# Attention stage: GpSimd's sums and lower halves of the key and query products spread over several units, finishing steps moved to units 68 to 79, output weights loaded before the key stores

## The reference

```
a1 = attn(q, k1, v1, causal=True)      # latent
a2 = attn(q, ks, vs, causal=False)     # 64 selected tokens
a3 = attn(q, kw, vw, causal=True)      # window
out = g[:,0]*a1 + g[:,1]*a2 + g[:,2]*a3
```

## Time and profile before

| | us |
|---|---|
| median of 3 runs | 2634.81 (2633.99 to 2637.43) |
| the profiled execution, its own time | 2636.5 |
| its span in the profile | 2634.8 |
| PE busy (PEld busy) | 2237.9 (1863.9) |
| DVE, ACT, POOL busy | 1877.2, 1720.0, 1758.6 |

### The profile page before, as it was taken

One profiled execution on the slowest core, in us unless ns is written; L12 is line 12 of the kernel. 1 busy time (PEld: TensorE's weight loads), 2 busy tenths in 40 slices (PEclk: granted clock), 3 DMA queues, 4 the chain that ended last, 5 costly groups with the idle time before them and its releaser, 6 DMA issues. The chain is left out here.

```text
span 2634.8 us, 37397 instructions
## 1 busy us (share of the span) xinstructions
PE 2237.9 (85%) x11394; PEld 1863.9 (71%) x11394; DVE 1877.2 (71%) x3720; ACT 1720.0 (65%) x3574; POOL 1758.6 (67%) x1544
## 2 busy tenths in 40 slices
PE   0178578999999999999999999999999994839885
PEld 0165437887878788787878878788888883728885
DVE  2656467687887878787787878788888873555553
ACT  3433216787877878777787777788888883216663
POOL 4154516778787877878787787877878774017884
PEclk9975569999999999999999999999999997759998
DMA  9767726345252434425342542322412203426776
GB/s 380 327 204 236 224 62 166 75 91 133 62 137 74 93 86 96 119 75 134 77 93 76 107 111 63 94 43 55 80 34 55 44 16 87 140 83 189 194 197 169
DMA packets 199860, 314.81 MB, mean 119 GB/s; under 512 B 95915, under 2 KB 130219, under 8 KB 186731
## 3 DMA queue, kind: packets, MB, share of 16 engines
q1 hardware_dynamic: 189947, 298.23, 40.6%
q0 software_dynamic: 9712, 14.18, 2.9%
HBM read 210.20 MB, written 101.75 MB: 118 GB/s over the span
## 5 line engine op out<-in xcount | busy, mean ns | idle before, releaser
L1418 POOL TENSOR_TENSOR p_lo<-prob,p_hi 128x512 fp32r<-128x512 f32 (+3 forms) x1072 | 1232.6, 1169 | 396.6 <-ACT p_hi L1502 368.4
L1500 ACT ACTIVATE prob<-ps_s 128x512 f32<-128x512 f32 (+4 forms) x1344 | 727.2, 541 | 380.8 <-DVE ps_s L1736 208.8
L1502 ACT ACTIVATE p_hi<-ps_s 128x512 fp32r<-128x512 f32 (+3 forms) x1344 | 726.3, 540 | 1.6
L1634 DVE TENSOR_REDUCE max_part<-ps_x 128x1 f32<-128x512 f32 x744 | 506.7, 687 | 108.5 <-PE ps_x L1546 98.2
L1632 DVE CUSTOM_DVE_ANT_0 ps_x<-ps_x,before 128x128 f32<-128x128 f32 x496 | 244.0, 492 | 30.5 <-PE ps_x L1546 22.0
L1599 PE MATMUL ps_o<-p_hi,v_lat 128*128 128x512 f32 (+3 forms) x640 | 240.3, 376 | 26.0 <-POOL p_lo L1418 25.9
L1599 PE MATMUL ps_o<-p_hi,v_win 128*128 128x512 f32 (+3 forms) x640 | 238.0, 372 | 2.7 <-POOL p_lo L1418 2.7
L1601 PE MATMUL ps_o<-p_lo,v_lat 128*128 128x512 f32 (+3 forms) x640 | 237.8, 372 | 0.0
L1601 PE MATMUL ps_o<-p_lo,v_win 128*128 128x512 f32 (+3 forms) x640 | 235.2, 367 | 0.0
L1418 DVE TENSOR_TENSOR p_lo<-prob,p_hi 128x512 fp32r<-128x512 f32 (+1 forms) x208 | 207.7, 999 | 10.8 <-ACT p_hi L1502 10.7
L1736 DVE TENSOR_TENSOR ps_s<-ps_s,mask_kq 128x128 f32<-128x128 f32 x512 | 150.2, 300 | 74.2 <-PE ps_s L1518 65.6
(11 more groups left out here) (433 smaller groups left out, 5823.6 us busy)
## 6 DMA issues: line engine op xcount, KB each, us to landing
raw<-in_experts_w_dram SPq DMA_DIRECT2D x23, 1536.0 KB
wbuf<-in_tok_weight_dram SPq DMA_DIRECT2D x16, 2000.0 KB, 16.9
head_first<-kw_scratch SPq DMA_DIRECT2D x72, 256.0 KB, 5.0
kw_scratch<-st_hi SPq DMA_DIRECT2D x48, 256.0 KB, 2.3
kw_scratch<-st_lo SPq DMA_DIRECT2D x48, 256.0 KB, 3.0
q_scratch<-st_hi SPq DMA_DIRECT2D x48, 256.0 KB, 4.4
q_scratch<-st_lo SPq DMA_DIRECT2D x48, 256.0 KB, 5.1
head_first<-q_scratch SPq DMA_DIRECT2D x48, 256.0 KB, 6.0
```

Of the source, the lines that this page charges most:

```text
L1418: ns.tensor_tensor(upper if low else p_lo[:, i % LSLOTS, c:CH], prob[low:P, i % NPROB, c:CH], upper.bitcast(F32), ALU.subtract).then_inc(s ...
L1500: nc.scalar.activation(prob[low:P, i % NPROB, c:CH], ps_s[i % 3][low:P, c:CH], ACT.Exp, scale=SCALE).then_inc(s["p_full"], 1)
L1502: nc.scalar.activation(p_hi[:, i % SLOTS, c:CH], ps_s[i % 3][:, c:CH], ACT.Exp, scale=SCALE).then_inc(s["p_up"], 1)
L1634: ins = nc.vector.tensor_reduce(mpart[:, q, c:c + 1], bank[:, 0:w], axis=AX.X, op=ALU.max)
```

## The change

It does six things.

1. `turn_sum`: the difference stays one unit after part 2, the sum goes two units after it (`SUM_LAG`). ACT rounds the first two units after part 2 and the second three after (`UP_LAG`). POOL's lower halves come four and five units after it (`LOW_LAG`); all of these came one, two and three units after.
2. `SPLIT_W` goes from unit 60 to 72, so POOL's split of the next head's values goes from 62 to 74.
3. `LO_DVE`: units 66, 72 and 78 go to POOL, units 63, 79, 81 and 82 to DVE.
4. `FINISH`: steps 1 to 5 go to units 68, 70, 73, 76 and 79.
5. SP stores the inverse and loads the weights before the key stores, and no longer behind them.
6. DVE holds the task of a query's part 0 back by one unit, when it is the only task of its unit: it comes behind the next unit's cut.

```diff
-SPLIT_L, SPLIT_W = 20, HU + 16
+SPLIT_L, SPLIT_W = 20, HU + 28
+SUM_LAG, UP_LAG, LOW_LAG = (1, 2), (2, 2, 3), (3, 4, 5)
-LO_DVE = sorted(CAUSAL[2::6] + [i for i in range(NU) if UNITS[i][0] == SELECT])
+LO_DVE = sorted([2, 9, 15, 22, 28, 35, 42, 48, 54, 60, 63, 79, 81, 82] + [i for i in range(NU) if UNITS[i][0] == SELECT])
...
                 store_sums(h, 0)
+                if h:
+                    store_inverse(h - 1)
+                    load_weight(h - 1)
                 if ahead:
                     store_out(*PIN[h + 1], "kw", 0)
                     if h + 2 < len(PIN):
                         load_kw_inputs(h + 2)
                     store_out(*PIN[h + 1], "kw", 1)
                     store_out(*PIN[h + 1], "kw", 2)
-                if h:
-                    store_inverse(h - 1)
-                    load_weight(h - 1)
...
                     if i == SPLIT_W + 2 and h + 1 < H:
                         split_low(h + 1, WINDOW)
-                    for t in AT.get((h, i - 1), ()):
-                        turn_sum(pool, t)
+                    for r in range(2):
+                        for t in AT.get((h, i - SUM_LAG[r]), ()):
+                            turn_sum(pool, t, r)
                     if i in LO_POOL:
                         lower(pool, h, i)
-                    for t in AT.get((h, i - 3), ()):
-                        turn_low(pool, t)
+                    for part in range(3):
+                        for t in AT.get((h, i - LOW_LAG[part]), ()):
+                            turn_low(pool, t, part)
...
-                    for t in AT.get((h, i - 2), ()):
-                        if t[0] != "prep" or t[2] != "q" or t[4]:
-                            round_up(act, t)
+                    for t in AT.get((h, i - UP_LAG[0]), ()):
+                        if t[2] == "kw":
+                            round_up(act, t, 0)
+                    for part in (1, 2):
+                        for t in AT.get((h, i - UP_LAG[part]), ()):
+                            round_up(act, t, part)
...
-        FINISH = {HU + 6: 0, NU - 8: 1, NU - 6: 2, NU - 5: 3, NU - 4: 4, NU - 2: 5}
+        FINISH = {HU + 6: 0, NU - 16: 1, NU - 14: 2, NU - 11: 3, NU - 8: 4, NU - 5: 5}
...
+            held = [()]
...
-                    for t in AT.get((h, i), ()):
+                    for t in held.pop(0):
+                        dve_task(dve, t)
+                    tasks = AT.get((h, i), ())
+                    wait = i + 1 < NU and len(tasks) == 1 and tasks[0][0] == "prep" and tasks[0][2] == "q" and tasks[0][4] == 0
+                    held.append(tasks if wait else ())
+                    for t in () if wait else tasks:
                         dve_task(dve, t)
```

More of the change, by code:

```diff
@@ L1390, in _, with turn_sum, turn_low @@
             sp.wait_ge(s["store"], 16 * H)
-        def turn_sum(pool, t):
+        def turn_sum(pool, t, r):
             if t[0] == "prep" and t[4] == 2:
-                n = out_number(t, 1)
-                pool.wait_ge(s["turn"], batch(t) + 1)
-                for r, (x, y, op) in enumerate(((0, 2, ALU.subtract), (1, 3, ALU.add))):
-                    full_free(pool, n + r)
-                    nc.gpsimd.tensor_tensor(full[:, (n + r) % NO, :], turned[:, x, :], turned[:, y, :], op).then_inc(s["back"], 1)
-        def turn_low(pool, t):
-            if t[0] == "prep" and not (t[2] == "q" and t[4] == 0) and t[4] != 1:
-                for part in ((0,) if t[4] == 0 else (1, 2)):
-                    n = out_number(t, part)
-                    pool.wait_ge(s["up"], n + 1)
-                    nc.gpsimd.tensor_tensor(st_lo[:, n % NO, :], full[:, n % NO, :], st_hi[:, n % NO, :].bitcast(F32), ALU.subtract).then_inc(s["low_pool"], 1)
+                n = out_number(t, 1) + r
+                x, y, op = ((0, 2, ALU.subtract), (1, 3, ALU.add))[r]
+                if r == 0:
+                    pool.wait_ge(s["turn"], batch(t) + 1)
+                full_free(pool, n)
+                nc.gpsimd.tensor_tensor(full[:, n % NO, :], turned[:, x, :], turned[:, y, :], op).then_inc(s["back"], 1)
+        def turn_low(pool, t, part):
+            if t[0] == "prep" and t[4] == (2 if part else 0) and (part or t[2] == "kw"):
+                n = out_number(t, part)
+                pool.wait_ge(s["up"], n + 1)
+                nc.gpsimd.tensor_tensor(st_lo[:, n % NO, :], full[:, n % NO, :], st_hi[:, n % NO, :].bitcast(F32), ALU.subtract).then_inc(s["low_pool"], 1)
         def lower(eng, h, i):
@@ L1492, in _ @@
                     for t in AT.get((h, i - 1), ()):
-                        if t[0] == "prep" and t[2] == "q" and t[4] == 0:
-                            round_up(act, t)
+                        if t[2] == "q":
+                            round_up(act, t, 0)
                     if i in DIAG:
```

8 lines of the change are left out of this document (3 added, 5 removed).

## The result

The changed kernel takes 2601.06 us (median of 4 runs, 2599.06 to 2601.53) against 2634.7 for the kernel before (4 runs, 2633.99 to 2637.43): a ratio of 0.9871, 95% interval 0.9858 to 0.9883. It is faster by 34 us. The forecast was 55 us less; the time lies in the range, but 21 us above the forecast. The profiled execution took 2601.53 us, its span is 2599.8.

What follows compares the result with a forecast made beforehand. PE was taken as the bound, its waits mostly for POOL's lower halves. Terms 41.2 + 11.0 + 5.5 + 2.4 + 2.0 - 7.5 = 54.6 us less gave 2580.2 us against the median of 2634.8; range 2555 to 2620.

Steps and rivals of the forecast that it cites:

- The key projection: Main term: edits 1 and 2 remove PE's waiting and slow clock there, 39.0 us in ten heads plus 2.2 in head 0.
- Part 0: Query part 0, heads 1 to 11: edit 6 removes PE's wait of 1.0 us a head, 11.0 us.
- Parts 1 and 2: Query parts 1 and 2, heads 1 to 11: edit 1 shortens the wait for POOL by 0.5 a head, 5.5 us.
- The end of the head: Edits 3 and 4 take the additions from there, so ACT is less late: 0.6 us in four heads, 2.4 us.
- Rival 2: The query's waits only move, so its two terms, 16.5 us, are lost: 2597 us; chance 0.11.
- Head 0: First 24 units, with two projections: POOL's work in smaller groups gains 2 us, between 0 and 6.
- GpSimd in units 68 to 77: Cost of added GpSimd work: 0.6 us in heads 1 to 10, 0.3 in heads 11 to 15, 7.5 us in all.
- the first rival: GpSimd becomes the bound in units 68 to 77, costing 50 us in place of 7.5: 2623 us; chance 0.14.
- The spare: Time from unit 68's lower half being ready to PE using it: about 2.7 us, against GpSimd falling 2.3 behind.
- rival 4: The weights still come late and DVE waits at the first product, some 4 us a head: about 2633 us; chance 0.02.
- Rival 3: DVE starves beside a pauseless POOL, two blocks of 3.8 us in each of heads 1 to 15: 2687 us; chance 0.05.

Runs made afterwards that it cites:

- Experiment 8: The kernel before with only edits 1 and 5 (the lags and the earlier weight loads): 2595.9 us.
- 11: Changed kernel with the cast at unit 53, split at 54, lower halves of 63, 72, 78 on VectorE, 66, 79, 81, 82 on GpSimd: 2575.0 us.
- 12: As 11, with unit 81's lower half on VectorE too: 2563.4 us, ratio 0.9729 to the kernel before.
- experiment 7: The changed kernel with edit 6 undone, so the query's part 0 is not held back: 2607.2 us.
- 6: The changed kernel with the cast at unit 55, the split at 57, unit 72's lower half on VectorE and unit 79's on GpSimd: 2587.5 us.
- 10: The changed kernel with the split at 57 and edit 3 undone (the old list of lower halves): 2584.3 us.

## Why the prediction was right or wrong

**The key projection: right.** 41.2 was forecast. PE's loss at units 60 to 71 went from 4.0 to 0.05 in heads 1 to 10, 40 us, and in head 0 its wait of 2.4 us went too. The clock stayed at 1.00. The shares were less right: I put all of it down to the lags and the split (edits 1 and 2). Experiment 8 shows that the lags alone give 2.5 of the 4.0. The other 1.5 went with the split at 74 or 54 and, in the list, unit 63 on DVE and 66 off it (the changed kernel, 11 and 12); with the split at 57 and the old list 1.6 was left, with the changed list 0.7. That edit 3 gives something here, I hadn't counted.

**The query and the end of the head: right in sum, wrong in shares.** Forecast 11.0 + 5.5 + 2.4 = 18.9. Part 0 gave 0.55 x 11 = 6 (experiment 7). Parts 1 and 2 gave 1.2 - 0.6 in eleven heads, 6. The end of the head gave 0.7 to 0.8 at the start of fourteen heads, some 10: I had taken it that the query's matmuls cover it in heads 1 to 11, and they don't. Together 22. Rival 2 didn't come.

**Head 0.** Forecast 2. It gained 4.5 in units 12 to 23, 0.8 in 24 to 35 and 2.5 at unit 66, and lost 3.4 in its first units, where the wait for the transfer is 3.2 us longer, and 0.6 at its end. That its 4.1 us in all are near the 2 and the 2.2 of the key projection that I had charged is luck.

**GpSimd in units 68 to 77: wrong, and this is the failing step.** I charged 0.6 and 0.3 us a head, 7.5 in all; it is 2.6 in heads 1 to 10, 2.3 in heads 11 to 14 and 0.6 in head 0, some 36. (Head 15, without a split, loses 2.5 by another cause, below.) That is the first rival's mechanism at some 36 of the 50 us that I gave it, without the slow clock that I had in it. The step has four parts:

- *The work* was right: 15.3 us was forecast for the split and ten lower halves. From the end of unit 68's lower half to the end of unit 78's, GpSimd works 15.3 us in head 13 and 15.4 in head 5.
- *PE's time* was wrong. I set 13.0 against it, the length of the stage in which the scores of these units are made. But a lower half is wanted four units later, when PE is at units 72 to 81, which are quicker. From the products of unit 68 to those of unit 78, before, PE needs 11.85 us, not 13.0:

```profile
1995.30 0.40 PE L1599 MATMUL ps_o<-p_hi,v_lat 128*128 128x512 f32 x1
```

- *Idle time* was left out: 0.95 + 0.26 us in head 13, in which GpSimd waits for `p_hi`, since ACT has a read, the cast and a late cut before unit 72. In head 5 there is none.
- *The spare* at unit 68 was forecast at 2.7 for both kinds of head. It is 2.7 in heads 11 to 14, but only 1.3 in heads 1 to 10. There GpSimd was to be done with unit 68 14.0 us after the beginning of the difference, and PE to use it at 16.7 (my terms for the first add up to 13.7 and not to 14.0); measured in head 5, it is 15.1 and 16.4. GpSimd is idle for 0.80 before unit 62 and takes 2.98 us for the two `st_lo`, not 2.55.

With both sides laid over the same stretch, from unit 68 to unit 78, the account closes. In head 13 GpSimd takes 16.5 us with its idle time, PE 11.85: a debt of 4.7, less the spare of 2.7, leaves 2.0, and the product of unit 78 does come 13.85 us behind that of unit 68 (1963.87 - 1950.02), 2.0 later than before. In head 5 it is 15.4 - 11.85 - 1.3 = 2.3, and 14.2 - 11.85 = 2.35 measured. The 0.3 that is left in either comes at units 82 and 83.

Two slips in the rivals changed nothing. The row of the loads says 1.75 us for all four and not for each, and the sum of rival 4 leaves out the charge of 7.5; by my own terms it would be 2640.

**The sum by heads** closes for heads 1 to 10: -4.0 - 0.55 - 0.75 - 0.55 + 2.6 = -3.25, measured -3.2; and for heads 12 to 14: -0.75 + 2.3 = +1.5, measured +1.5.

**Rival 3** came once in the changed kernel, in head 15, whose GpSimd has no split. Timelines there of DVE, of POOL and of PE:

```profile
2156.52 5.17 DVE L1716 TENSOR_TENSOR raw_o<-raw_o,o_weight 128x512 f32<-128x512 f32 x1
```

```profile
2152.36 8.78 POOL L1419 TENSOR_TENSOR p_lo<-prob,p_hi 128x512 fp32r<-128x512 f32 x7
```

```profile
2162.98 0.50 PE L1518 MATMUL ps_s<-q_hi,k_hi 99*128 99x512 f32 x1 [2.28 <-ACT p_hi L1503]
```

The product is held for 5.17 us, the cut behind it is late, ACT with it, and PE stands for 2.28. In heads 1 to 14 the products took 0.7 to 1.9 and the additions 0.9 to 1.4, and the rival's two blocks a head didn't come. It came in a smaller form, 0.3 to 1.0 us in some of the heads, once the debt was gone (experiments 6, 10, 11 and 12).

## What to carry to other kernels

A debt and a spare must be laid over the same instructions: count the time of a feeding engine from unit m to unit n, its idle time included, and the time of the engine that it feeds from the use of unit m to the use of unit n, which may be several units and another kind of unit later. And read the spare in each kind of turn: here it was 2.7 in one and 1.3 in the other. Work taken from a tight place goes where the spare is largest and nothing tight follows soon; debt at the end of a loop's body isn't paid there, it is carried into the next turn. And when a change has one part with the gain and others that make room for it, try the first part alone: here the lags alone were as good as the whole. When a wait goes, see also who made it: a long instruction next to it may be another delay.
